# Activation transposes moved from TensorE to transposing DMAs, shifted rows issued by ScalarE, order of work replaced

## What is computed

```python
def _layer(x, wqkv, qs, ksc, wo, lg, lb, w1, b1, w2, b2):
    h = shift_token(x)                      # second half of the columns comes from the row before
    q, k, v = jnp.split(h @ wqkv, 3, axis=-1)
    q, k = l2norm(q) * qs, l2norm(k) * ksc  # per head, 8 heads of 64
    q, k = rotary_xpos(q, k)
    o = local_attention(q, k, v)            # own window of 128 rows and the one before
    x = x + o @ wo
    h = shift_token(x)
    h = layer_norm(h) * lg + lb             # mean and variance over the shifted row
    a, g = jnp.split(h @ w1 + b1, 2, axis=-1)
    return x + (a * gelu(g)) @ w2 + b2
```

## Time and profile before

| | |
|---|---|
| median of 3 runs | 2639.29 us (2638.84 to 2642.74) |
| span of the profiled execution | 2634.1 us |
| median less that span | 5.2 us |
| PE (TensorE matmul) busy | 2526.7 us, 96% |
| DVE (VectorE) busy | 2260.9 us, 86% |
| ACT (ScalarE) busy | 1935.6 us, 73% |
| POOL (GpSimd) busy | 1303.7 us, 49% |
| instructions | 71297 |

### The profile page before, as it was taken

One profiled execution on the slowest core, in us unless ns is written; L12 is line 12 of the kernel. 1 busy time (PEld: TensorE's weight loads), 2 busy tenths in 40 slices (PEclk: granted clock), 3 DMA queues, 4 the chain that ended last, 5 costly groups with the idle time before them and its releaser, 6 DMA issues.

```text
span 2634.1 us, 71297 instructions
## 1 busy us (share of the span) xinstructions
PE 2526.7 (96%) x25566; PEld 1725.1 (65%) x25566; DVE 2260.9 (86%) x6247; ACT 1935.6 (73%) x4782; POOL 1303.7 (49%) x953
## 2 busy tenths in 40 slices
PE   7899989999899998999999999999999999999998
PEld 4566666666567665676656666666766666666675
DVE  8997889878898788987889878998889978799785
ACT  3698856888478784788748787587874878658884
POOL 2364535555355554555436554365544555446552
PEclk8999999999999999999999999999999999999999
DMA  5000010000100000000000000000000000000000
GB/s 192 22 7 8 5 43 3 9 5 15 33 3 9 6 17 30 4 10 4 18 29 5 8 5 20 25 6 8 6 19 25 6 8 6 20 25 6 7 6 21
DMA packets 51021, 46.45 MB, mean 18 GB/s; under 512 B 11530, under 2 KB 47980, under 8 KB 50548
## 3 DMA queue, kind: packets, MB, share of 16 engines
q1 hardware_dynamic: 50004, 40.78, 5.0%
q10 hardware_dynamic: 672, 1.10, 0.1%
HBM read 25.06 MB, written 8.42 MB: 13 GB/s over the span
## 4 chain that ended last, share of the span: by engine, by line
PE 69%; DVE 12%; ACT 8%; issue 5%; POOL 4%; DMA 1%; SPq 1%; DVEq 0%; POOLq 0%; ACTq 0%
PE ps L508 10%; PE ps L613 9%; PE ps L581 8%; PE ps L547 6%; PE ps L514 5%; PE ps L617 4%; PE ps L565 4%; PE ps L524 3%; PE ps L594 3%; PE ps L160 2%; PE ps L162 2%; PE ps L161 2%; ACT ar_b L808 2%; PE ps L461 2%; PE ps L407 2%
## 5 line engine op out<-in xcount | busy, mean ns | idle before, releaser
L808 ACT ACTIVATE ar_b<-ar_b,small 128x192 f32<-128x192 f32 (+1 forms) x1024 | 445.2, 437 | 50.4 <-DVE small L1100 48.6
L1366 POOL TENSOR_TENSOR small<-small,neg_half 128x16 f32<-128x16 f32 x128 | 382.2, 2986 | 121.8 <-DVE small L1059 119.9
L1370 POOL TENSOR_TENSOR ar_c<-ar_c 128x1024 f32<-128x1024 f32 x128 | 302.7, 2365 | 282.3 <-DVE ar_c L1086 281.7
L1100 DVE CUSTOM_DVE_ANT_0 ar_b<-ps,mask_t,small 128x192 f32<-128x192 f32 x896 | 319.3, 413 | 29.7 <-PE ps L547 29.2
L1385 POOL TENSOR_TENSOR mlp<-mlp 128x512 f16<-128x512 f32 x160 | 196.3, 1231 | 200.5 <-ACT mlp L863 199.3
L508 PE MATMUL ps<-wqkv_hi,ht_hi 128*128 128x512 f16 x768 | 292.2, 381 | 0.0
L508 PE MATMUL ps<-wqkv_lo,ht_hi 128*128 128x512 f16 x768 | 291.1, 379 | 0.0
L613 PE MATMUL ps<-ht_hi,w_hi 128*128 128x512 f16 (+1 forms) x704 | 268.2, 381 | 5.5 <-ACT ht_hi L759 5.5
L613 PE MATMUL ps<-ht_hi,w_lo 128*128 128x512 f16 (+1 forms) x704 | 267.1, 379 | 0.0
L581 PE MATMUL ps<-ar_b,ar_a 128*64 128x128 f32 x3840 | 239.4, 276 | 0.5 <-DVE ar_b L1124 0.3
L294 POOL TENSOR_SCALAR stats<-stats 128x2 f32<-128x2 f32 x128 | 33.2, 260 | 407.6 <-DVE stats L1149 312.5
(11 more groups left out here) (193 smaller groups left out, 6673.3 us busy)
## 6 DMA issues: line engine op xcount, KB each, us to landing
xu<-in_L_attn_x_dram SPq DMA_DIRECT2D x32, 256.0 KB, 2.8
out_dram<-xu SPq DMA_DIRECT2D x64, 128.0 KB, 2.4
rows<-xu SPq DMA_DIRECT2D x128, 63.5 KB
mlp<-in_L_ffn_wqkv_dram SPq DMA_DIRECT2D x2, 1536.0 KB, 6.4
modb<-mod_rows SPq DMA_DIRECT2D x8, 384.0 KB, 4.5
rows<-in_L_ffn_w_dram SPq DMA_DIRECT2D x2, 1364.0 KB, 9.5
rows<-xu SPq DMA_DIRECT2D x112, 0.5 KB
ar_b<-in_L_wmod_dram SPq DMA_DIRECT2D x2, 768.0 KB, 7.4
```

The source lines that it names most:

```text
L808: last = act.activation(pw, pw, ACT.Exp, bias=mnw[:, n % 2, h:h + 1], scale=-1.0, accum_out=smw[:, n % 2, h:h + 1])
L1100: dve.tensor_tensor_reduce(out=PW[:, pw_at(f, q, i) + c:pw_at(f, q, i) + KW], in0=ps[:, bk, i * KW + c:(i + 1) * KW], in1=mask, scale=rinv ...
L1366: pool.tensor_tensor(rinv[:, n % 4, :], ssm[:, n % 2, :], neg_half[:, 0:16], ALU.pow).then_inc(s_rinv, 1)
L1370: pool.tensor_tensor(M1[:, n % 2, :], M1[:, n % 2, :], M2, ALU.add).then_inc(s_add, 1)
```

## The change

The transposes `D` and `N` leave TensorE. `dh` and `dl` now make the high and the low part from the rows, in the row layout, in a new buffer `d_rows` (float16, [128, 2 tiles, 2 parts, 256]), and `nh` and `nl` the same in `n_rows`, for which `XN` gives up its second buffer. `D` and `N` become pieces of SyncE: after `dl` or `nl`, two `dma_start_transpose` of [128, 512] float16 each, 128 KB, write both parts of a tile into `ht_all`. They wait for what `dh` and `nh` waited for before, that the last readers of `ht` are done. `E`, `Wg` and `Wa` wait for the landing. `dh` and `nh` of a pair wait on ScalarE until the pair before it has landed, since there is one buffer. `xs` moves from SyncE to ScalarE with both its DMAs and its wait for `jr`. Two PSUM bank uses per pair of tiles go. All of `BEGIN`, `ONCE`, `EDGE` and `PERIOD` are replaced; the diff below keeps those lines of the tables that the prediction speaks of.

```diff
-        ht = [sb(f"ht_{s}", [P, NC, SEQ + 1], F16) for s in ("hi", "lo")]
...
+        ht_all = sb("ht", [P, 2, NC, HT0 + SEQ], F16)
+        ht = [ht_all[:, s] for s in range(2)]
...
+        d_rows = sb("d_rows", [P, 2, 2, DIM], F16)
...
-        XN = rows[:, 0:1024].rearrange("p (r t n) -> p r t n", r=2, t=2)
+        XN = rows[:, 0:512].rearrange("p (t n) -> p t n", t=2)
+        n_rows = rows[:, 512:1024].bitcast(F16).rearrange("p (t s n) -> p t s n", t=2, s=2)
...
+        h_landed = lambda L: 16 * (4 * L + 2)
+        ln_landed = lambda L: 16 * (4 * L + 4)
...
-                    elif k == "xs":
-                        n = piece[1]
-                        l, w = n // NT % DEPTH, n % NT
-                        sp.wait_ge(s_res, at("jr", n))
-                        if n == 0:
-                            sp.wait_ge(s_rows, 1)
-                        sp.dma_start(XS[1:P, w, :], U[0:P - 1, w, P:DIM]).then_inc(s_xs[l * 4 + w // 2], 16)
-                        if w + 1 < NT:
-                            sp.dma_start(XS[0:1, w + 1, :], U[P - 1:P, w, P:DIM]).then_inc(s_xs[l * 4 + (w + 1) // 2], 16)
+                    elif k == "D":
+                        L, p = piece[1:]
+                        sp.wait_ge(s_dl, at("dl", L, p))
+                        if L % DEPTH:
+                            sp.wait_ge(s_w1g, at("Wg", L - 1, p // 2, NJ))
+                            sp.wait_ge(s_w1, at("Wa", L - 1, p // 2, NJ - 1))
+                        else:
+                            sp.wait_ge(s_proj, at("pj", L // DEPTH, 2 * p + 1))
+                        for t in range(2):
+                            c = HT0 + (2 * p + t) * P
+                            sp.dma_start_transpose(ht_all[:, :, :, c:c + P].rearrange("p s c n -> p (s c) n"),
+                                                   d_rows[:, t].rearrange("p s n -> p (s n)")).then_inc(s_hT[p], 16)
+                    elif k == "N":
+                        L, p = piece[1:]
+                        sp.wait_ge(s_nl, at("nl", L, p))
+                        for k2 in range(3):
+                            sp.wait_ge(s_qkv, at("E", L * NT + min(2 * p + 2, NT - 1), k2))
+                        for t in range(2):
+                            c = HT0 + (2 * p + t) * P
+                            sp.dma_start_transpose(ht_all[:, :, :, c:c + P].rearrange("p s c n -> p (s c) n"),
+                                                   n_rows[:, t].rearrange("p s n -> p (s n)")).then_inc(s_hT[p], 16)
...
-                    elif k == "D":
-                        L, p = ids
-                        if L % DEPTH:
-                            pe.wait_ge(s_u2, at("yr", (L - 1) * NT + 2 * p + 1))
-                        else:
-                            pe.wait_ge(s_u0, at("lr", L // DEPTH, 2 * p + 1))
-                        bk = claim(pe, *piece)
-                        rows_t(bk, lambda t: U[:, 2 * p + t, :]).then_inc(s_dt, 1)
-                    elif k == "N":
-                        L, p = ids
-                        pe.wait_ge(s_xnw, at("lk", L, p))
-                        bk = claim(pe, *piece)
-                        rows_t(bk, lambda t: XN[:, p % 2, t, :]).then_inc(s_nt, 1)
...
+                        if w and w % 2 == 0:
+                            pe.wait_ge(s_hT[w // 2 - 1], h_landed(L))
+                        pe.wait_ge(s_hT[w // 2], h_landed(L))
...
-                        pe.wait_ge(s_nh, at("nh", L, 2 * g + 1))
+                        for p in (2 * g, 2 * g + 1):
+                            pe.wait_ge(s_hT[p], ln_landed(L))
...
-                        act.wait_ge(s_dt, at("D", L, p))
                         if L % DEPTH:
-                            act.wait_ge(s_w1g, at("Wg", L - 1, p // 2, NJ))
-                            act.wait_ge(s_w1, at("Wa", L - 1, p // 2, NJ - 1))
+                            act.wait_ge(s_u2, at("yr", (L - 1) * NT + 2 * p + 1))
                         else:
-                            act.wait_ge(s_proj, at("pj", L // DEPTH, 2 * p + 1))
-                        act.activation(ht[0][:, :, 1 + p * 256:1 + (p + 1) * 256],
-                                       ps[:, bank["D", L, p], :].rearrange("p (c n) -> p c n", c=NC),
-                                       ACT.Copy).then_inc(s_dh, 1)
+                            act.wait_ge(s_u0, at("lr", L // DEPTH, 2 * p + 1))
+                        if L or p:
+                            M, q = divmod(L * 4 + p - 1, 4)
+                            act.wait_ge(s_hT[q], h_landed(M))
+                        act.activation(d_rows[:, :, 0, :], U[:, 2 * p:2 * p + 2, :], ACT.Copy).then_inc(s_dh, 1)
                     elif k == "nh":
...
-                        act.wait_ge(s_nt, at("N", L, p))
-                        for k2 in range(3):
-                            act.wait_ge(s_qkv, at("E", L * NT + min(2 * p + 2, NT - 1), k2))
-                        act.activation(ht[0][:, :, 1 + p * 256:1 + (p + 1) * 256],
-                                       ps[:, bank["N", L, p], :].rearrange("p (c n) -> p c n", c=NC),
-                                       ACT.Copy).then_inc(s_nh, 1)
+                        act.wait_ge(s_xnw, at("lk", L, p))
+                        if L or p:
+                            M, q = divmod(L * 4 + p - 1, 4)
+                            act.wait_ge(s_hT[q], ln_landed(M))
+                        act.activation(n_rows[:, :, 0, :], XN, ACT.Copy).then_inc(s_nh, 1)
...
+                    elif k == "xs":
+                        n, = ids
+                        l, w = n // NT % DEPTH, n % NT
+                        act.wait_ge(s_res, at("jr", n))
+                        if n == 0:
+                            act.wait_ge(s_rows, 1)
+                        act.dma_start(XS[1:P, w, :], U[0:P - 1, w, P:DIM]).then_inc(s_xs[w // 2], 16)
+                        if w + 1 < NT:
+                            act.dma_start(XS[0:1, w + 1, :], U[P - 1:P, w, P:DIM]).then_inc(s_xs[(w + 1) // 2], 16)
...
+                    elif k == "dl":
...
+                        dve.tensor_tensor(d_rows[:, :, 1, :], U[:, 2 * p:2 * p + 2, :], d_rows[:, :, 0, :],
+                                          ALU.subtract).then_inc(s_dl, 1)
+                    elif k == "nl":
+                        L, p = ids
+                        dve.wait_ge(s_nh, at("nh", L, p))
+                        dve.tensor_tensor(n_rows[:, :, 1, :], XN, n_rows[:, :, 0, :], ALU.subtract).then_inc(s_nl, 1)
...
-                        if L or p >= 2:
-                            dve.wait_ge(s_nt, at("N", *divmod(L * 4 + p - 2, 4)))
+                        if L or p:
+                            dve.wait_ge(s_nl, at("nl", *divmod(L * 4 + p - 1, 4)))
...
-PERIOD = 316.98
+PERIOD = 322.4
...
-    ("os", "sp"): {0: 345.6, 1: 346.12, 2: 346.64, 3: 347.16, 4: 347.68, 5: 348.2, 6: 348.72, 7: 349.24},
...
-    ("ls", "dve"): {(0, 0): 116.67, (0, 1): 129.1, (0, 2): 168, (0, 3): 184.03, (1, 0): 242.83, (1, 1): 258.16,
-        (1, 2): 301.33, (1, 3): 310.67},
...
-    ("xs", "sp"): {0: 96.44, 1: 106.95, 2: 120.45, 3: 124.39, 4: 149.38, 5: 162.39, 6: 174.87, 7: 179.27, 8: 216.76,
-        9: 231.21, 10: 247.44, 11: 253.45, 12: 287.13, 13: 290.43, 14: 300.56, 15: 305.96},
...
+    ("D", "sp"): {(0, 0): 76.91, (0, 1): 98.59, (0, 2): 119.61, (0, 3): 126.38, (1, 0): 205.43, (1, 1): 222.59,
+        (1, 2): 270.94, (1, 3): 289.08},
...
+    ("N", "sp"): {(0, 0): 162.51, (0, 1): 175.47, (0, 2): 212.94, (0, 3): 238.37, (1, 0): 284.23, (1, 1): 302.84,
+        (1, 2): 351.77, (1, 3): 358.36},
...
+    ("E", "pe"): {(0, 0): 80.76, (0, 1): 82.91, (0, 2): 93.01, (1, 0): 88.29, (1, 1): 103.62, (1, 2): 102.32,
...
+    ("os", "sp"): {0: 335.07, 1: 336.82, 2: 341.74, 3: 347.07, 4: 384.51, 5: 386.53, 6: 389.31, 7: 392.42},
...
+    ("Wa", "pe"): {(0, 0, 0): 179.32, (0, 0, 1): 183.22, (0, 0, 2): 184.52, (0, 0, 3): 185.82, (0, 0, 4): 194.4,
+        (0, 1, 0): 246.65, (0, 1, 1): 247.95, (0, 1, 2): 249.25, (0, 1, 3): 252.45, (0, 1, 4): 253.75,
+        (1, 0, 0): 313.63, (1, 0, 1): 314.93, (1, 0, 2): 317.97, (1, 0, 3): 319.87, (1, 0, 4): 325.33,
+        (1, 1, 0): 362.21, (1, 1, 1): 363.95, (1, 1, 2): 366.37, (1, 1, 3): 374.17, (1, 1, 4): 375.47},
...
+    ("ls", "dve"): {(0, 0): 156.06, (0, 1): 169.87, (0, 2): 207.85, (0, 3): 233.22, (1, 0): 272.91, (1, 1): 297.11,
+        (1, 2): 342.95, (1, 3): 352.72},
...
+    ("xs", "act"): {0: 139.81, 1: 149.83, 2: 162.52, 3: 167.96, 4: 180.08, 5: 205.94, 6: 226.73, 7: 231.19, 8: 261.03,
+        9: 270.13, 10: 290.46, 11: 295.2, 12: 326.16, 13: 340.69, 14: 347.65, 15: 350.51},
...
-    ("za", "act"): {(): -30.17},
...
+    ("za", "act"): {(): 0},
```

150 lines of the change are left out of this document (66 added, 84 removed), and 813 rows, old and new, of tables (BEGIN, EDGE).

## The result

The changed kernel takes 2995.54 us (median of 4 runs, 2988.73 to 2998.32) where the kernel before takes 2639.79 (4 runs): a ratio of 1.134, 95% interval 1.133 to 1.136, 356 us slower. The forecast was 2740, with a range up to 2870. The sign was right, the size was not.

What follows compares the result with a forecast made beforehand. TensorE was taken as the bound, 97% busy with 9.7 us idle per sequence. The sum was 2634 + 33 (order) + 43 (shifted rows) + 25 (ScalarE issue) = 2735, as median 2740 us (+3.8%), range 2640 to 2870.

Steps and rivals of the forecast that it cites:

- What is removed: TensorE: 128 groups of four transposes leave, each holding its place 0.42 us; 54 us of the span, 6.7 per sequence.
- What replaces it: SyncE: a pair of transposing DMAs per group, taken to land in 3.85 us, within 2.9 to 8.7.
- What the order gives: New table of due times: 51 us longer than the old; span between 2649 and 2685, middle 2667, so +33.
- The shifted rows: VectorE's statistics: transfer takes 5.17 us, new table leaves as little as 1.91; +43 us (0 to 85).
- The issue on ScalarE: ScalarE: row issues hold it 18.8 us per sequence beyond the table, 150 in all; a sixth taken, +25 (0 to 150).
- (c): Rival: TensorE's idle time does not grow and its 54 us come out whole; 2585, halfway 2612; chance 0.13.
- (d): Rival: the transposes leave TensorE, but hand-overs eat exactly what they gave; 2639; chance 0.04.
- (a): Rival: the order holds as written, shifted rows and issues fall into TensorE's waits; 2672; chance 0.22.
- (b): Rival: transposing DMAs take the upper bound, 4.85 us late nine times per sequence, 175 us halved; 2915; chance 0.14.
- What would show it: Expected profile after: TensorE busy 54 to 78 us less, idle 20 us or more per sequence, sequence 331 to 335 us.

Runs made afterwards that it cites:

- e10: Kernel before with the new table of due times, transposes still on TensorE, shifted-row transfers left out: 2858.84 us (1.083).
- e6: Changed kernel without transposing DMAs and without shifted-row transfers, products reading what the buffer holds: 2792.65 us (1.059).
- e9: Kernel before in its own order, shifted-row transfers and VectorE's wait for them taken out: 2636.16 us (0.999).
- e1: Changed kernel without any shifted-row transfer, neither issue nor wait: 2814.0 us (1.067).
- e2: Changed kernel, shifted rows issued on ScalarE, but statistics and norm read the unshifted rows; only a tile's last residual sum waits: 2906.84 us (1.102).
- e12: Changed kernel in the old table, casts, subtractions and transposing DMAs placed by a rule, shifted rows issued by SyncE: 2933.94 us (1.112).
- e11: Changed kernel without transposing DMAs and shifted-row transfers, VectorE's clamp written as tensor_reduce instead of tensor_scalar: 2777.38 us (1.052).
- e14: Kernel before with only the statistics of the shifted rows due 2.8 us earlier in the table: 2746.32 us (1.041).
- e17: Changed kernel with rows sent as 112 and 15 by SyncE, clamp as tensor_reduce, and new x's statistics and norm due 3 us earlier: 2892.78 us (1.095).
- e7: Kernel before with the new table of due times, transposes on TensorE, shifted rows issued by SyncE: 2957.85 us (1.122).
- e5: Changed kernel without the transposing DMAs, products reading what the buffer holds, shifted rows kept: 2962.13 us (1.123).
- e8: Kernel before with one edit, shifted rows issued by ScalarE at their old due times: 2742.7 us (1.040).

## Why the prediction was wrong

The runs form a chain from one kernel to the other, each step one change, but for e10 to e6, where several go together. "Idle" and "clock" are TensorE's per sequence, worked out as in the first table.

| step | us | difference | idle | clock |
|---|---|---|---|---|
| before | 2639 | | 9.7 | 2.1 |
| no shifted rows (e9) | 2636 | -3 | 9.7 | 1.8 |
| the new order (e10) | 2859 | +223 | 22.6 | 9.3 |
| no transposes at all (e6) | 2793 | -66 | 22.3 | 9.8 |
| the transposing DMAs (e1) | 2814 | +21 | 23.9 | 10.6 |
| rows issued on ScalarE (e2) | 2907 | +93 | 32.7 | 12.4 |
| and waited for (after) | 2996 | +89 | 42.6 | 16.9 |

Between e10 and e6 the row casts also take the place of the copies out of PSUM, and copies and subtractions go back to the changed kernel's due times. By e10 the order costs 223 us; by e6 it is 157 with the 54 us of transposes taken out, so 211, casts included. Of the 24 us that e10 adds to a sequence, idle time and clock account for 20; the two columns are rough.

By the prediction's own steps:

- **"What is removed", 54 us.** Right in size: 6.7 us a sequence in the first table, give or take 4, and 66 us in the chain, which has the casts in it too.
- **"What replaces it", at 3.85 us.** Right for an undisturbed pair, 3.8 us; among the kernel's other transfers the median is 4.2, and one pair in ten takes 6.4 or more, which the sum had at nothing. In the new order all of it costs 21 to 33 us. The estimate from the Trainium skill's "VectorE: DVE Perf Modes", section "The three transpose paths" (10.5 us for a pair, 2979 us), came close to the time for a reason that is not there: no pair took more than 7.8. It was also right that such a hand-over needs other work in front of it; without that it costs what e12 shows.
- **"What the order gives", +33. This is the step that failed.** The kernel that has this term and not the two below it, new order and transposing DMAs and no shifted rows, is e1: +175 us (2814), and so 142 of the 256 us that the forecast was short. I took the difference of two table lengths (51 us) as a bound for the new order, on the footing that the table would miss the trace by 36 us again, or by nothing. e1 misses its 2649 by 162. A table of due times says nothing of how well its order stands lateness: e10 has no shifted rows, and its order costs 223. Of the 24 us a sequence more, 12.9 are idle time of TensorE and 7.5 the clock behind it, for which the sum had no term at all; VectorE and GpSimd in each other's way are part of the cause, 15 us of it by e11.
- **"The shifted rows", +43 of 0 to 85.** The mechanism was right: the transfer mostly still takes 5.2 to 5.3 us from issue to reader, up to 7.7 where two are issued close together, and VectorE waits 185 us, at seven places of a sequence. (By the packet records 3.4 us of the 5.2 are moving, not 2.9, and the old table's 4.71 us, read as its slack, is only that of its tightest places.) The size was not: 89 us, which is 46 of the shortfall, and 107 in the old order by e14. I took half of the four places where nothing stands between the rows and TensorE. The timeline at 1509 shows what was left out: behind `ls` in VectorE's queue stands also work of the next sequence, for which TensorE waits.
- **"The issue on ScalarE", +25 of 0 to 150.** A sixth was taken, since ScalarE is idle 81 us a sequence. Measured 93 us, 68 above the term, and 105 in the old order: about two thirds of the 150 us by which the issues exceed the table. Idle time elsewhere doesn't hide an issue that stands in front of an exponential or a copy. The Trainium skill's "DMA: Bandwidth & Descriptors", section "Issuing engines are not separate DMA queues", finds the issue time saved by a second issuer usually small against the transfer; per transfer that holds here too (0.6 and 1.0 us against 5.2), but what stands behind the issues paid for them, and the sum by that rule, 2715, was the farther off.
- **Rivals.** (c) and (d) fell with the sign, (a) with every term. (b) had nearly the size, 2915, but from the transposing DMAs, which were cheap.
- **What would show it.** L407 is gone, idle time is over 20 us, the issues take 0.6 and 1.0 us and the first products wait for transposing pairs. But the shifted rows' wait is 23 us a sequence in place of 14, a sequence takes 362 us in place of 331 to 335, and TensorE's busy time rose by 73 us where it was to fall by 54 to 78, because the low clock had been left out.

What stays open: where the order loses its 154 us in e6, of which the clamp of e11 explains 15. TensorE's wait for the norm of x is its largest piece by name (52.5 us in e6), but the one attempt on it, e17, ran into the load of x. The account by idle time and clock says how the time is lost, not which pieces ought to stand elsewhere.

## What to carry to other kernels

In an order that is written out by hand and runs at 97% of its bound, price a late piece by everything that stands behind it in its queue, up to the next wait of the bounding engine, and don't halve it because that engine's neighbours show idle time: here 2.8 us taken from the table at eight places cost 107 us, and 1.5 us of issue per tile 93 to 105. Test a new order apart from a new method, by running the old instructions in it; that one run (e7) made 320 of the 356 us. Before moving a piece, look at the load in front of it, and move that too (e17). Repairs that hide behind each other have to be tried together.

## What the runs showed of the hardware

- A DMA from SBUF to SBUF of 112 partitions by 512 bytes landed in 1.9 us, and one of 127 partitions took 5.2 us from issue to reader at 22 GB/s. Two issues, 112 and 15 rows, are faster than one: VectorE's wait fell from 185.2 to 34.6 us. Two of 127 rows issued 2.9 us apart run one behind the other, and the second takes 6.3 to 7.7 us to its reader (seven sequences each of e5 and the profile after).
- A transposing DMA of 128 KB (128 rows of 512 two-byte numbers) landed in 2.5 us, holding SyncE's queue 1.27 us, and kept all sixteen DMA engines busy: the windows from 1512 to 1516 show DMA shares of 1.04 and 0.90. Its longest landing was 7.2 us. A pair, issued back to back, took 3.8 us in the median without the shifted rows beside it (e1) and 4.2 with them.
- A VectorE `tensor_scalar` of 128x16 took 174 ns at least and up to 1.32 us beside a GpSimd instruction, ending with it. The same size as `tensor_reduce` took 169 to 173 ns every time. How often they meet goes with the order: the mean is 240 ns in the old, 427 to 462 in the new, 244 in e12, the new method in the old order.
- The granted clock went to 0.50 in idle stretches of TensorE and stayed there some microseconds after it had resumed. The missed clock is 2.1 us a sequence before and 16.9 after, with 33 us more of idle time. That is no fixed price: in e8 TensorE has 10 us more idle time a sequence than before, in short pieces (its two longest groups of waits are 21.2 us in 21 and 20.9 us in 26), and misses 2.8 us of clock in place of 2.1.
